# First attention of a two-block kernel: q and k in two float32r parts, 50 rows per head, two heads stacked on one array

## The chip, the cores and the metric

The kernel runs on one core of one Trainium2 chip. The metric is the device time of one execution in microseconds (us). Engines are named as the profile names them: PE (matmuls), PEld (PE's weight loads), DVE, ACT, POOL and SP, which issues most of the DMAs.

## What is computed

The input x has 8 images of 128 channels and 32 x 32 positions, so T = 1024 positions per image. The whole is an attention block, a mixture of experts, a convolutional linear attention and a second mixture of experts, each added to x. The change touches only the first attention and the stage that feeds it:

```python
xn = groupnorm(channelnorm(x))                 # [8, 128, 1024]
q, k, v = split(qkv_w @ xn + qkv_b, 3)         # 8 heads of 16 channels
q, k = q * scale, k * scale                    # scale = 1/2
weight = softmax(einsum('bct,bcs->bts', q, k)) # 64 heads, 1024 x 1024, float32
a = einsum('bts,bcs->bct', weight, v)
x = x + proj_w @ (xn + a) + proj_b
```

## The kernel before, in words

**Stages.** `metaformer` runs stages one after the other, with a barrier between two of them. `normalize_and_project` (from L51) makes q, k and v of every image and stores them to DRAM. `attend_and_route_first` (from L360) computes the attention and the routing of the first mixture. Experts, convolution, second routing and second mixture follow; the change leaves them as they are.

**Stage 1.** Per image, PE projects; ACT adds the bias to q and k (L184). Each is then split into three bf16 parts whose sum is the value to float32's accuracy: a copy on ACT gives the first part, a subtraction gives a rest (`split_rest`, L227; DVE has q, POOL has k), ACT copies the rest into the second part (L200), and a second subtraction, `split_last` (L232; again DVE q, POOL k), gives the third. ACT's L200 and `split_last` run in the next image's turn. DVE also copies v from the banks and normalizes. SP stores the parts (L109 to L113), 768 KB for each of q and k and image. Behind the first image's store, SP loads image 0's stacks from DRAM (L118), 12 transfers.

**The stacks.** A product of q and k in parts is a sum over six pairs of parts. `Q_PARTS` and `K_PARTS` list them (0,0), (0,1), (0,2), (1,0), (1,1), (2,0), and both operands hold them under each other: 6 x 16 = 96 rows (`KB`) of bf16, eight heads side by side on the free axis. Rows 96 to 98 (`KM` = 99) carry the row maxima: in `ks` they are ones, in `qs` the negated maximum of each query in three bf16 parts, so that a score leaves PE with its maximum already subtracted. POOL sets the ones (L1054) at the start of the attention stage.

**Two products.** A *maximum* (`take_max`, L550) multiplies 128 queries by 512 keys over 96 rows into a bank, and DVE's `reduce` (L779) takes the maximum over the keys. There are 256 units (8 heads, 8 chunks of queries, 2 halves of the keys) per image; after each 64 units DVE merges the halves and negates. PE transposes the result (`rows`, L543), DVE copies it (L789), POOL's `split_rows` (`split_in_three`, four operations, L40 to L48) makes the parts, and SP shifts them into `qs` (`max_rows`, L467, three transfers). A *score* (L652) is 128 keys by 512 queries over 99 rows; ACT takes the exponential of two of them at once (L726) into P; `weigh` (L632) multiplies P by v, eight float32 products on 32-column tiles of the array, two rounds of four heads.

**The order of the work.** The attention of one image is a body of 32 steps. Each step has two pairs of scores for two pairs of heads; behind each pair stand other units from the list `BODY_UNITS` (L326): this image's maxima from the 80th on, the next image's first 80 (`LEAD`), and for the image before the two projections (L557 and L559), the turns (L605), the logits (L611) and the ranks (L618). `STEP_OF` spreads the 264 units over the 32 steps by their place in the list. The first two units of a step come behind the first pair of scores, the others behind the second, and the weighing of the step before ends a step (L671). A unit takes one of three banks in turn, `slot = 5 + index % 3`, and waits until the unit three places ahead is done with it:

```python
pe.wait_ge(unit_freed, base + max(index - 2, 0))
```

Ahead of the first body the first 80 maxima run by themselves. SP loads the next image's stacks in two halves while a body runs (`load_qk`, L457).

Of the kernel before, what the change touches and what calls it, by code (L numbers as in the profile page):

```python
# [6 lines left out]
F32 = mybir.dt.float32  # L7
BF16 = mybir.dt.bfloat16
ALU = mybir.AluOpType
ACT = mybir.ActivationFunctionType  # L10
AX = mybir.AxisListType
# [10 lines left out]
Q_PARTS = (0, 0, 0, 1, 1, 2)  # L22
K_PARTS = (0, 1, 2, 0, 1, 0)
KB = len(Q_PARTS) * CH
KM = KB + 3
# [9 lines left out]
def split_in_three(eng, value, rest, parts, done, b, held=None):  # L35


    if held is not None:
        eng.sem_inc(held, 1)
    eng.tensor_copy(parts[:, 0], value).then_inc(done, 1)  # L40
    eng.wait_ge(done, b * 4 + 1)
    eng.tensor_tensor(rest, value, parts[:, 0], ALU.subtract).then_inc(done, 1)
    eng.wait_ge(done, b * 4 + 2)
    if held is not None:
        eng.sem_inc(held, 1)
    eng.tensor_copy(parts[:, 1], rest).then_inc(done, 1)
    eng.wait_ge(done, b * 4 + 3)
    eng.tensor_tensor(parts[:, 2], rest, parts[:, 1], ALU.subtract).then_inc(done, 1)  # L48


def normalize_and_project(nc, sb, sem, bank, w, X, XF, stacks0, parts_dram, v_dram):  # L51
# [9 lines left out]
    rest = sb("rest", [C, 2, T], F32)  # L61
    parts = sb("parts", [C, 2, 2, 3, T], BF16)
# [18 lines left out]
    first_parts, second_parts = sem("first_parts"), sem("second_parts")  # L81
    q_rest, k_rest, q_split, k_split = sem("q_rest"), sem("k_rest"), sem("q_split"), sem("k_split")
# [21 lines left out]
    with nc.Block() as block:  # L104
        @block.sync
        def _(sp):
# [10 lines left out]
            sp.wait_ge(parts_stored[0], 32)  # L117
            for r, (qp, kp) in enumerate(zip(Q_PARTS, K_PARTS)):  # L118
                for s, part, stack in ((0, qp, stacks0[0]), (1, kp, stacks0[1])):
                    sp.dma_start(stack[r * CH:(r + 1) * CH], parts_dram[0, s, part].rearrange("(h i) t -> i h t", i=CH)).then_inc(stacks_loaded, 16)  # L120
# [3 lines left out]
            sp.wait_ge(stacks_loaded, 16 * 2 * len(Q_PARTS))  # L124
# [48 lines left out]
        def _(act):  # L173
# [3 lines left out]
            def project(b, s):  # L177

                if s == 0:
                    act.wait_ge(q_rest, b)  # L180
                    act.wait_ge(k_rest, b)
# [5 lines left out]
            def step(db, b, nb, cb, p):  # L187
# [9 lines left out]
                if db is not None:  # L197
                    for s, rest_ready in enumerate((q_rest, k_rest)):
                        act.wait_ge(rest_ready, db + 1)
                        act.activation(parts[:, 1 - p, s, 1], rest[:, s], ACT.Copy).then_inc(second_parts, 1)  # L200
# [2264 lines left out]
```

## Time and profile before

| | before |
|---|---|
| median of 3 runs | 2270.06 us (2269.89 to 2271.42) |
| the profiled execution's own time | 2275.42 us |
| its span | 2273.5 us |
| mean granted clock of PE | 0.916 |
| PE busy | 1929.1 us, 85% of the span |
| PEld busy | 1073.3 us, 47% |
| DVE busy | 1436.2 us, 63% |
| ACT busy | 1098.7 us, 48% |
| POOL busy | 755.4 us, 33% |

The span is that of one execution taken by the profiler; what lies outside it is 1.9 us. Busy shares are means over stages with different limits, so a stage has to be read by itself. A busy PE counts matmuls whose records can overlap. The granted clock is a share of 2.4 GHz, 0.50 being 1.2 GHz. In the rows, "out<-in" gives the program's names, and the brackets behind a group are its idle time and what ended it.

### The profile page before, as it was taken

What the parts mean: (1) busy time and instruction counts of PE and PEld (TensorE: products, weight loads), DVE (VectorE), ACT (ScalarE), POOL (GpSimd) and SP (SyncE); (2) the same over time, 40 slices, a digit from 0 to 9 for tenths busy, and PEclk for the clock granted to TensorE, in tenths of its full rate; (3) what the DMA queues carried; (4) which work ended last, traced back from release to release, by engine and by line L of the source; (5) the groups of instructions that cost most, each with busy time, mean ns of one, the idle gap of its engine ahead of it and who ended that gap; (6) DMA issues with size and microseconds to landing.
All of it is one profiled execution on the core that took longest, in us unless ns stands there. A gap on an engine that the chain in (4) does not pass through costs nothing. (4 is left out here: it accounts for less than half of the span.)

```text
span 2273.5 us, 41046 instructions
## 1 busy us (share of the span) xinstructions
PE 1929.1 (85%) x13306; PEld 1073.3 (47%) x13307; DVE 1436.2 (63%) x3154; ACT 1098.7 (48%) x1682; POOL 755.4 (33%) x883
## 2 busy tenths in 40 slices
PE   5769999999999999998589996996659992699993
PEld 2331223332332323232367774554447661599992
DVE  4769888888888888871346665762235665344444
ACT  4550665666666666666144442541225551344442
POOL 0232003343333333345335553000001667355551
PEclk9875999999999999999699998999879996799995
DMA  3851532323232323012333333322100242233326
GB/s 127 193 217 33 78 55 29 60 35 65 31 66 29 66 29 66 2 38 63 105 86 99 95 99 119 111 84 61 38 29 29 62 136 81 71 94 92 90 72 229
DMA packets 134782, 180.00 MB, mean 79 GB/s; under 512 B 44592, under 2 KB 87856, under 8 KB 132336
## 3 DMA queue, kind: packets, MB, share of 16 engines
q1 hardware_dynamic: 116208, 138.25, 25.6%
q0 software_dynamic: 18432, 39.88, 5.2%
q8 instruction: 87, 1.43, 0.3%
q14 instruction: 55, 0.45, 0.1%
HBM read 99.04 MB, written 69.01 MB: 74 GB/s over the span
## 5 line engine op out<-in xcount | busy, mean ns | idle before, releaser
L779 DVE TENSOR_REDUCE mx<-bank 128x1 f32<-128x512 f32 x1024 | 639.7, 696 | 86.4 <-PE bank L550 85.2
L726 ACT ACTIVATE P<-bank 128x1024 f32<-128x1024 f32 x512 | 497.4, 1021 | 313.1 <-PE bank L652 312.9
L550 PE MATMUL bank<-ks,qs 96*128 96x512 bf16 x1024 | 358.6, 402 | 35.5 <-DVE mx L779 35.5
L1290 POOL DMA_INDIRECT results<-yo,places x284 | 274.1, 965 | 283.6 <-DVE yo L1280 236.8
L652 PE MATMUL bank<-qs,ks 99*128 99x512 bf16 x1024 | 308.2, 384 | 2.6 <-ACT P L726 1.8
L1206 PE MATMUL bank<-xt,up 128*128 128x256 f32 x1136 | 274.8, 386 | 3.7 <-DVE xt L1257 1.4
L632 PE MATMUL bank<-P,vt 128*32 128x512 f32 x2048 | 272.8, 605 | 0.7 <-ACT P L726 0.7
L2289 POOL DMA_INDIRECT dispatched<-planes,places x128 | 124.5, 973 | 420.2 <-DVE stats L2133 357.3
L1206 PEld LDWEIGHTS bank<-xt,up 128*128 128x128 f32 x1136 | 207.5, 193 | 30.4 <-issue 4.7
L550 PEld LDWEIGHTS bank<-ks,qs 96*128 96x128 bf16 x1024 | 99.8, 98 | 257.5 <-DVE mx L779 177.7
L652 PEld LDWEIGHTS bank<-qs,ks 99*128 99x128 bf16 x1024 | 78.0, 97 | 280.0 <-ACT P L726 182.8
L1237 ACT ACTIVATE hidden<-bank,rec 128x256 f32<-128x256 f32 x284 | 125.3, 473 | 144.3 <-PE bank L1206 144.3
L999 POOL TENSOR_TENSOR a<-o,den 128x512 f32<-128x512 f32 x32 | 40.6, 1268 | 381.4 <-ACT den L714 381.4
L1275 DVE TENSOR_TENSOR y<-bank,rec 128x256 f32<-128x256 f32 x142 | 60.3, 425 | 132.7 <-PE bank L1215 131.5
L1215 PE MATMUL bank<-planes,hidden 128*128 x1136 | 138.6, 276 | 0.7 <-DVE y L1275 0.7
L1049 POOL DMA_INDIRECT dispatched<-outgoing,places x128 | 123.8, 967 | 44.9 <-issue 39.9
L1215 PEld LDWEIGHTS bank<-planes,hidden 128*128 128x128 f32 x1136 | 132.5, 192 | 1.0 <-issue 0.9
L1717 PE MATMUL bank<-planes,bands 32*32 32x240 f32 (+2 forms) x3840 | 86.0, 396 | 41.6 <-issue 26.5
L1242 ACT ACTIVATE gate<-bank,rec 128x256 f32<-128x256 f32 x142 | 67.2, 473 | 111.1 <-PE bank L1206 111.1
L1738 DVE STREAM_TRANSPOSE planes<-out 128x1024 f32<-128x1024 f32 x24 | 43.6, 1894 | 98.6 <-ACT out L1730 98.6
L1189 PE MATMUL bank<-weights,xr 128*128 128x128 f32 x284 | 55.2, 277 | 47.8 <-DMA xr<-dispatched 47.1
L1269 DVE SCALAR_TENSOR_TENSOR hidden<-bank,rec,gate 128x256 f32<-128x256 f32 x142 | 68.6, 484 | 40.8 <-ACT gate L1242 31.0
(298 smaller groups left out, 2581.8 us busy)
## 6 DMA issues: line engine op xcount, KB each, us to landing
xr<-dispatched SPq DMA_DIRECT2D x142, 130.0 KB
qk_parts<-parts SPq DMA_DIRECT2D x16, 768.0 KB, 5.1
qs<-qk_parts SPq DMA_DIRECT2D x84, 128.0 KB
ks<-qk_parts SPq DMA_DIRECT2D x84, 128.0 KB
v_turned<-vt SPq DMA_DIRECT2D x8, 1024.0 KB, 5.6
vt<-v_turned SPq DMA_DIRECT2D x8, 1024.0 KB
bands<-results SPq DMA_DIRECT2D x32, 256.0 KB, 3.7
y<-results SPq DMA_DIRECT2D x32, 256.0 KB
```

What stands on the lines that cost most here:

```text
L550: pe.matmul(bank[:, slot, :], qs[par][0:KB, h, c * C:(c + 1) * C], ks[par][0:KB, h, half * HALF:(half + 1) * HALF], start=True, stop=True) ...
L632: ins = pe.matmul(bank[32 * j:32 * j + 32, 4, :], vt[:, par, s, head * VH:(head + 1) * VH], P[:, (2 * e + j // 2) % SLOTS, j % 2 * HALF:(j ...
L652: ins = pe.matmul(bank[:, 2 * pair + u, :], ks[par][:, head, s * C:(s + 1) * C], qs[par][:, head, n * HALF:(n + 1) * HALF], start=True, st ...
L726: act.activation(P[:, x % SLOTS, :], bank[:, 2 * pair:2 * pair + 2, :] .rearrange("p a t -> p (a t)"), ACT.Exp).then_inc(probs_ready, 1)
L779: dve.tensor_reduce(mx[:, k // 2, k % 2:k % 2 + 1], bank[:, slot, :], AX.X, ALU.max).then_inc(unit_freed, 1)
L1049: pool.indirect_dma_start(xd_dram, bass.IndirectOffsetOnAxis(places[:, q, k:k + 1], 0), outgoing[:, q, k, :], None).then_inc(sent, 16)
L1206: ins = pe.matmul(bank[:, 2 + f, 0:SLOT], up[:, p, f * C:(f + 1) * C], xt[:, p, :], start=True, stop=True)
L1215: ins = pe.matmul(bank[:, 6 + p, q * C:(q + 1) * C], hidden[:, p, f, q * C:(q + 1) * C], weights(e, W2 + f * C), start=(f == 0), stop=(f = ...
L1237: act.activation(hidden[:, p, f, :], bank[:, 2 + f, 0:SLOT], ACT.Gelu, bias=rec[:, r, f:f + 1]).then_inc(h_ready, 1)
L1290: pool.indirect_dma_start(yd_dram, bass.IndirectOffsetOnAxis(places[:, p, q:q + 1], 0), yo[:, p, q, :], None).then_inc(sent[p], 16)
L1717: ins = pe.matmul(sums[:, :, y0:y1], bands[rows, m * TAPS + dy, :], plane[:, :, y0 + dy - PAD:y1 + dy - PAD], start=(dy == DY_ORDER[0]), s ...
L2289: pool.indirect_dma_start(xd_dram, bass.IndirectOffsetOnAxis(places[:, p, q, k:k + 1], 0), rows[p][:, q, k, :], None).then_inc(sent[p], 16)
```

## The change

q and k are split into two parts in float32 storage, read as float32r by PE: the copy into the first part rounds to float32r, one subtraction gives the second. Three pairs of parts remain, 48 rows (`KB`) per head, and two rows of maxima make 50 (`KM`). One head's rows lie at partitions 0 to 49, the other's at 64 to 113 (`stack_rows`, `ROWS` = 64), so a stack has four pairs of heads on the free axis and 4096 float32 elements per partition where it had 8192 bf16. Maxima are counted so that units 2j and 2j + 1 are the same chunk of two stacked heads (`maximum`); `STEP_OF` goes by pairs, so both are in one step, and `first_half` puts two maxima or one other unit behind the first pair of scores. Each maximum still waits for its own unit's bank. Ones: stage 1's POOL sets those of one parity at its start, the attention's POOL the other's.

Stage 1 and the units, cut (lines "..." mark what is left out; the loads, the shifts and the waits on their counts change with the layout):

```diff
-Q_PARTS = (0, 0, 0, 1, 1, 2)
-K_PARTS = (0, 1, 2, 0, 1, 0)
+Q_PARTS = (0, 0, 1)
+K_PARTS = (0, 1, 0)
 KB = len(Q_PARTS) * CH
-KM = KB + 3
+KM = KB + 2
+PAIRS = HEADS // 2
+ROWS = C // 2
...
+    eng.tensor_copy(parts[:, 0].bitcast(F32R), value).then_inc(done, 1)
+    eng.wait_ge(done, b * 2 + 1)
+    eng.tensor_tensor(parts[:, 1].bitcast(F32R), value, parts[:, 0], ALU.subtract).then_inc(done, 1)
...
-    parts = sb("parts", [C, 2, 2, 3, T], BF16)
+    parts = sb("parts", [C, 2, 2, 2, T], F32)
...
+                    for u in range(2):
+                        sp.dma_start(stack[stack_rows(u, r)],
+                                     parts_dram[0, s, part].rearrange("(p u i) t -> u i p t", u=2, i=CH)[u]).then_inc(stacks_loaded, 16)
...
-                        act.activation(parts[:, 1 - p, s, 1], rest[:, s], ACT.Copy).then_inc(second_parts, 1)
...
-            eng.tensor_tensor(rest[:, s], qk[:, s], parts[:, p, s, 0], ALU.subtract).then_inc(rest_ready, 1)
-
-        def split_last(eng, s, b, p, split):
-
-            eng.wait_ge(second_parts, b * 2 + s + 1)
-            eng.tensor_tensor(parts[:, p, s, 2], rest[:, s], parts[:, p, s, 1], ALU.subtract).then_inc(split, 1)
+            eng.tensor_tensor(parts[:, p, s, 1].bitcast(F32R), qk[:, s], parts[:, p, s, 0], ALU.subtract).then_inc(ready, 1)
...
+            for u in range(2):
+                pool.memset(stacks0[1][u * ROWS + 32:(u + 1) * ROWS], 1.0).then_inc(ones_set, 1)
...
-    units.insert(units.index(("max", MAXIMA - 1)) + 4, ("rows", 1))
-    units.insert(units.index(("max", MAXIMA // 2 - 1)) + 4, ("rows", 0))
+    units.insert(units.index(("max", MAXIMA - 1)) + 3, ("rows", 1))
+    units.insert(units.index(("max", MAXIMA // 2 - 1)) + 3, ("rows", 0))
...
-STEP_OF = {unit: index * STEPS // len(BODY_UNITS) for index, unit in enumerate(BODY_UNITS)}
+BODY_GROUPS = [unit for unit in BODY_UNITS if unit[0] != "max" or unit[1] % 2 == 0]
+STEP_OF = {unit: index * STEPS // len(BODY_GROUPS) for index, unit in enumerate(BODY_GROUPS)}
+STEP_OF.update({("max", k): STEP_OF["max", k - 1] for k in range(1, MAXIMA, 2)})
...
+    pair, c, half, u = k // 32, k // 4 % TC, k // 2 % 2, k % 2
...
+    return 2 if now and now[0][1][0] == "max" else 1
...
-                pe.matmul(bank[:, slot, :], qs[par][0:KB, h, c * C:(c + 1) * C],
-                          ks[par][0:KB, h, half * HALF:(half + 1) * HALF], start=True, stop=True).then_inc(unit_filled, 1)
+                pe.matmul(bank[:, slot, :], qs[par][rows, pair, c * C:(c + 1) * C].bitcast(F32R),
+                          ks[par][rows, pair, half * HALF:(half + 1) * HALF].bitcast(F32R), start=True, stop=True).then_inc(unit_filled, 1)
...
-                            ins = pe.matmul(bank[:, 2 * pair + u, :], ks[par][:, head, s * C:(s + 1) * C],
-                                            qs[par][:, head, n * HALF:(n + 1) * HALF], start=True, stop=True)
+                            ins = pe.matmul(bank[:, 2 * pair + u, :], ks[par][rows_of, 2 * g + pair, s * C:(s + 1) * C].bitcast(F32R),
+                                            qs[par][rows_of, 2 * g + pair, n * HALF:(n + 1) * HALF].bitcast(F32R), start=True, stop=True)
...
-                        for index, (kind, k) in now[:2] if pair == 0 else now[2:]:
+                        for index, (kind, k) in now[:first_half(now)] if pair == 0 else now[first_half(now):]:
...
-                for par in range(2):
-                    pool.memset(ks[par][KB:KM, :, :], 1.0).then_inc(ones_set, 1)
-                pool.wait_ge(ones_set, 2)
+                for u in range(2):
+                    pool.memset(ks[1][u * ROWS + 32:(u + 1) * ROWS], 1.0).then_inc(ones_set, 1)
+                    pool.wait_ge(ones_set, u + 1)
```

How PE's instructions stand now, at two places. The first is the start of a body, its first two steps. Before, on PE (L652 scores, L550 maxima, L632 the weighing):

```order
L652 MATMUL bank<-qs,ks 128x512 x2
L550 MATMUL bank<-ks,qs 128x512 x2
L652 MATMUL bank<-qs,ks 128x512 x2
L550 MATMUL bank<-ks,qs 128x512 x3
L632 MATMUL bank<-P,vt 32x512 x4
L652 MATMUL bank<-qs,ks 128x512 x2
L550 MATMUL bank<-ks,qs 128x512 x2
L652 MATMUL bank<-qs,ks 128x512 x2
L550 MATMUL bank<-ks,qs 128x512 x2
L632 MATMUL bank<-P,vt 32x512 x4
```

and with the change, where scores are L659, maxima L559 and the weighing L641:

```order
L659 MATMUL bank<-qs,ks 128x512 x2
L559 MATMUL bank<-ks,qs 128x512 x2
L659 MATMUL bank<-qs,ks 128x512 x2
L559 MATMUL bank<-ks,qs 128x512 x4
L641 MATMUL bank<-P,vt 32x512 x4
L659 MATMUL bank<-qs,ks 128x512 x2
L559 MATMUL bank<-ks,qs 128x512 x2
L659 MATMUL bank<-qs,ks 128x512 x2
L559 MATMUL bank<-ks,qs 128x512 x2
L641 MATMUL bank<-P,vt 32x512 x4
```

The first step has six maxima where it had five: two behind the first pair of scores, four behind the second. The second step has four in both. Over a body the five-maxima steps, seven of them, become seven of six.

The second place is on PE around the projection (L557 and L559 before, L566 and L568 with the change). Before, an ordinary step and then both halves of the projection in one step:

```order
L652 MATMUL bank<-qs,ks 128x512 x2
L550 MATMUL bank<-ks,qs 128x512 x2
L652 MATMUL bank<-qs,ks 128x512 x2
L550 MATMUL bank<-ks,qs 128x512 x2
L632 MATMUL bank<-P,vt 32x512 x4
L652 MATMUL bank<-qs,ks 128x512 x2
L557 MATMUL bank<-XF,weights 128x512
L559 MATMUL bank<-a,weights 128x512 x2
L557 MATMUL bank<-XF,weights 128x512
L559 MATMUL bank<-a,weights 128x512 x2
L652 MATMUL bank<-qs,ks 128x512 x2
L550 MATMUL bank<-ks,qs 128x512 x2
```

and with the change:

```order
L659 MATMUL bank<-qs,ks 128x512 x2
L559 MATMUL bank<-ks,qs 128x512 x2
L659 MATMUL bank<-qs,ks 128x512 x2
L566 MATMUL bank<-XF,weights 128x512
L568 MATMUL bank<-a,weights 128x512 x2
L641 MATMUL bank<-P,vt 32x512 x4
L659 MATMUL bank<-qs,ks 128x512 x2
L566 MATMUL bank<-XF,weights 128x512
L568 MATMUL bank<-a,weights 128x512 x2
L659 MATMUL bank<-qs,ks 128x512 x2
L559 MATMUL bank<-ks,qs 128x512 x2
L641 MATMUL bank<-P,vt 32x512 x4
```

The two halves of the projection stand in two neighbouring steps, each beside one pair of maxima, where both were in one step with two maxima behind them.

## Rows read from the trace of the kernel before

**Rows 1.** Windows: bounds, us; busy of PE, PEld, DVE, ACT, POOL; clock; DMA share; GB/s.

```profile
20.00:168.00 148.00, 104.19 (x271) 55.29 (x270) 102.24 (x168) 84.01 (x128) 35.36 (x16) 0.82 0.56 163
180.00:221.00 41.00, 40.55 (x70) 7.20 (x69) 40.97 (x71) 0.00 (x0) 3.52 (x5) 0.50 0.03 7
221.00:1056.00 835.00, 802.08 (x4339) 248.49 (x4338) 672.79 (x1312) 550.28 (x633) 269.28 (x397) 1.00 0.29 47
1556.00:1582.00 26.00, 18.85 (x895) 12.77 (x895) 4.15 (x3) 5.12 (x5) 0.00 (x0) 1.00 0.28 77
```

**Rows 2.** Groups of instructions, 220 to 1060 us: busy, mean ns of one | idle before.

```profile
L779 DVE TENSOR_REDUCE mx<-bank 128x1 f32<-128x512 f32 x949 | 590.6, 683 | 85.7 <-PE bank L550 84.4
...
L550 PE MATMUL bank<-ks,qs 96*128 96x512 bf16 x947 | 313.7, 385 | 30.2 <-DVE mx L779 30.2
L652 PE MATMUL bank<-qs,ks 99*128 99x512 bf16 x1024 | 308.2, 384 | 2.6 <-ACT P L726 1.8
...
L550 PEld LDWEIGHTS bank<-ks,qs 96*128 96x128 bf16 x946 | 91.5, 97 | 215.4 <-DVE mx L779 136.2 <-issue 0.6
...
L611 PEld LDWEIGHTS bank<-router,X 128*128 128x128 f32 x112 | 13.1, 192 | 0.0
```

**Rows 3.** Timeline of one ordinary step and one with five maxima: start, length, engine, group.

```profile
425.21 0.61 PE L652 MATMUL bank<-qs,ks 99*128 99x512 bf16 x2
...
425.65 0.60 PE L550 MATMUL bank<-ks,qs 96*128 96x512 bf16 x2
...
426.07 2.49 DVE L779 TENSOR_REDUCE mx<-bank 128x1 f32<-128x512 f32 x4 [0.44 <-PE bank L550]
...
426.82 0.10 PEld L550 LDWEIGHTS bank<-ks,qs 96*128 96x128 bf16 x1 [0.41 <-DVE mx L779]
...
427.14 1.07 PE L632 MATMUL bank<-P,vt 128*32 128x512 f32 x8
...
428.14 0.61 PE L652 MATMUL bank<-qs,ks 99*128 99x512 bf16 x2
...
429.04 3.08 DVE L779 TENSOR_REDUCE mx<-bank 128x1 f32<-128x512 f32 x5 [0.48 <-PE bank L550]
...
431.71 0.39 PE L652 MATMUL bank<-qs,ks 99*128 99x512 bf16 x1
```

**Rows 4.** Timeline of PE around the projection, turns and logits of a body.

```profile
557.88 0.60 PE L652 MATMUL bank<-qs,ks 99*128 99x512 bf16 x2
558.32 1.02 PE L557 MATMUL bank<-XF,weights 128*128 128x512 f32 x2
...
560.89 1.02 PE L557 MATMUL bank<-XF,weights 128*128 128x512 f32 x2
...
565.43 0.61 PE L652 MATMUL bank<-qs,ks 99*128 99x512 bf16 x2
...
571.88 0.60 PE L652 MATMUL bank<-qs,ks 99*128 99x512 bf16 x2
...
576.63 0.60 PE L652 MATMUL bank<-qs,ks 99*128 99x512 bf16 x2
```

**Rows 5.** Groups of the page: the convolution's products on 32 x 32 tiles.

```profile
L1717 PE MATMUL bank<-planes,bands 32*32 32x240 f32 (+2 forms) x3840 | 86.0, 396 | 41.6 <-issue 26.5
```

**Rows 6.** Groups of instructions, 0 to 170 us: the copies and subtractions of stage 1.

```profile
L232 POOL TENSOR_TENSOR parts<-rest,parts 128x1024 bf16<-128x1024 f32 x8 | 17.1, 2136 | 33.8 <-ACT parts L200 33.8
...
L200 ACT ACTIVATE parts<-rest 128x1024 bf16<-128x1024 f32 x16 | 16.0, 1049 | 20.9 <-DVE rest L227 20.9
...
L232 DVE TENSOR_TENSOR parts<-rest,parts 128x1024 bf16<-128x1024 f32 x8 | 9.7, 1217 | 1.1 <-ACT parts L200 1.1
```

**Rows 7.** DMA issues, 60 to 168 us: loads of image 0's stack, KB each, us to landing.

```profile
qs<-qk_parts SPq DMA_DIRECT2D x6, 256.0 KB, 15.2
```

**Rows 8.** Timeline at the start of the attention stage, 168 to 176 us.

```profile
168.32 13.81 POOL L1054 MEMSET ks<- 3x8192 bf16 x2 [6.12 <-POOLq L2319]
...
168.39 6.88 DVE L880 COPY base<-weights 128x8 f32<-128x8 f32 x1 [8.17 <-PEq L2319]
```

More of the change, by code:

```diff
@@ L8 @@
 BF16 = mybir.dt.bfloat16
+F32R = mybir.dt.float32r
 ALU = mybir.AluOpType
@@ L272, in step @@
                     copy_v(b, p, 1)
-                if db is not None:
-                    split_last(dve, 0, db, 1 - p, q_split)
                 if nb is not None:
@@ L289, in step @@
                     copy_v(b, p, 3)
-                    split_rest(dve, 0, b, p, q_rest)
+                    split(dve, 0, b, p, q_split)
             over_images(dve, step)
@@ L339, with maximum, first_half @@
 BODY_UNITS = units_of_a_body()
-STEP_OF = {unit: index * STEPS // len(BODY_UNITS) for index, unit in enumerate(BODY_UNITS)}
+BODY_GROUPS = [unit for unit in BODY_UNITS if unit[0] != "max" or unit[1] % 2 == 0]
+STEP_OF = {unit: index * STEPS // len(BODY_GROUPS) for index, unit in enumerate(BODY_GROUPS)}
+STEP_OF.update({("max", k): STEP_OF["max", k - 1] for k in range(1, MAXIMA, 2)})
+def maximum(k):
+    pair, c, half, u = k // 32, k // 4 % TC, k // 2 % 2, k % 2
+    return pair, c, half, u
+def first_half(now):
+    return 2 if now and now[0][1][0] == "max" else 1
 def of_next(unit):
@@ L463, in max_rows @@
             def max_rows(b, par, g):
-                sp.wait_ge(rows_split, b * 8 + 4 * g + 4)
-                for part in range(3):
-                    sp.dma_start(qs[par][KB + part:KB + part + 1, 4 * g:4 * g + 4, :]
-                                 .rearrange("p h (c t) -> p (h c) t", t=C),
-                                 nm_parts[:, part, :]).then_inc(rows_loaded, 16)
+                sp.wait_ge(rows_split, b * 4 + 2 * g + 2)
+                for u in range(2):
+                    for part in range(2):
+                        row = u * ROWS + KB + part
+                        sp.dma_start(qs[par][row:row + 1, 2 * g:2 * g + 2, :].rearrange("p h (c t) -> p (h c) t", t=C),
+                                     nm_parts[16 * u:16 * u + 16, part, :]).then_inc(rows_loaded, 16)
             def blank_rows_at(sp, n):
@@ L545, in take_max @@
             def take_max(b, par, k, slot):
-                h, c, half = k // 16, k // 2 % TC, k % 2
+                pair, c, half, u = maximum(k)
+                rows = slice(u * ROWS, u * ROWS + KB)
                 if k % 64 == 0:
                     pe.wait_ge(qk_loaded[k // 64], b * LOADS)
-                pe.matmul(bank[:, slot, :], qs[par][0:KB, h, c * C:(c + 1) * C],
-                          ks[par][0:KB, h, half * HALF:(half + 1) * HALF], start=True, stop=True).then_inc(unit_filled, 1)
+                pe.matmul(bank[:, slot, :], qs[par][rows, pair, c * C:(c + 1) * C].bitcast(F32R),
+                          ks[par][rows, pair, half * HALF:(half + 1) * HALF].bitcast(F32R), start=True, stop=True).then_inc(unit_filled, 1)
             def project(b, n, slot):
@@ L778, in reduce @@
                 dve.wait_ge(unit_filled, filled)
-                dve.tensor_reduce(mx[:, k // 2, k % 2:k % 2 + 1], bank[:, slot, :], AX.X, ALU.max).then_inc(unit_freed, 1)
+                pair, c, half, u = maximum(k)
+                row = 32 * (pair // 2) + 16 * u + 8 * (pair % 2) + c
+                dve.tensor_reduce(mx[:, row, half:half + 1], bank[:, slot, :], AX.X, ALU.max).then_inc(unit_freed, 1)
                 if k % 64 == 63:
@@ L2339, in metaformer @@
             with ExitStack() as first:
-                stacks0 = [allocator(first, nc.sbuf_tensor)(name, [KM, HEADS, T], BF16)[:] for name in ("qs0", "ks0")]
+                stacks0 = [allocator(first, nc.sbuf_tensor)(name, [C, PAIRS, T], F32)[:] for name in ("qs0", "ks0")]
                 stage(normalize_and_project, X, XF, stacks0, parts_dram, v_dram)
```

70 lines of the change are left out of this document (28 added, 42 removed).

## Prediction

> **What bounds the kernel now.** I read the table by stretches first [rows 1]. The first attention is its third line: from 221 to 1056 us, 835 of the 2273.5 us. There PE is busy for 802 us, DVE for 673, ACT for 550, at a granted clock of 1.00. A busy PE is no proof, since matmul records overlap, so I went on to the groups of instructions [rows 2] and to one step in the order of time [rows 3].
>
> An ordinary step (four scores L652, four maxima products L550, the weighing L632 of the step before) goes from 425.21 to 428.14 us: 2.93 us. DVE's four reductions take 2.49 of it. What sets its length is a chain through both engines [rows 3]: first scores at 425.21; first maximum product 0.44 later (two scores at 0.22); DVE starts 0.42 after that; the weight load of the fourth maximum product, which waits until the first reduction has freed its bank, another 0.75 later (426.82); the weighing 0.32 later; the next scores 1.00 later. 0.44 + 0.42 + 0.75 + 0.32 + 1.00 = 2.93. The scores of the second pair and the third maximum product lie beside the first reduction and cost nothing. A step with five maxima lasts 3.57: one more reduction of 0.60.
>
> **The change, part by part.** The sum is made against the profiled execution, 2275.42 us with a span of 2273.5; the median of the runs, 2270.06, is 5.4 lower.
>
> *Ordinary steps.* Each score and each maximum product now has 50 or 48 rows in float32r and a head's half of the array, heads in turn. I take one float32r product to stream as a bf16 one, 0.22 us, and the two of a pair to run beside each other. The nearest row for the second is the convolution, whose 3840 products on small tiles of the array are busy for 86.0 us together, 22 ns each against 396 ns of one [rows 5]; no run here shows it for halves. Of the chain only the first pair of scores gets shorter, by 0.22. Against it stands the weight load: one of 128 bf16 columns reads 97 ns, one of 128 f32 columns 192 [rows 2], and in two places of the chain nothing hides it: at the first scores after the weighing (other tile shape) and at the maximum that waits. I take the f32 row, since the elements have four bytes: 2 x 0.095 = 0.19. So 2.93 - 0.22 + 0.19 = 2.90, almost nothing. Ends: a load as short as bf16's gives 2.71; loads of a pair one after the other add another 0.10, 3.00.
>
> *Steps laid out anew.* Maxima now keep together in pairs, so a step has six where it had five. By the order a body had seven steps of five maxima, twenty of four, one of four with a transposition, and four with other units; now it has seven of six, eighteen of four, one of four with a transposition, and six with other units. A sixth reduction adds 0.60: 3.57 becomes 4.14, seven times +0.57 = +4.0. Eighteen ordinary steps at -0.03: -0.5. The projection had 2.93 + 7.55 with one ordinary step [rows 4]; now it has two steps, each 0.32 + 0.22 + 0.22 for the pairs, 2.57 for three f32 products (558.32 to 560.89), 1.00 for the weighing and two changes of tile shape at about 0.1: 4.5, together 9.0, so -1.5. Turns and logits had 4.75 + 2.93; now I estimate 2.8 and 3.9, -1.0. The two steps with a transposition or the ranks lose one product and two halves, about three times 0.2 each: -1.1. Sum per image 4.0 - 0.5 - 1.5 - 1.0 - 1.1 = -0.1. What a body gains where PE is the limit it loses in the steps of six, where DVE is. With eight bodies I put the attention at 0; by the ends of the load, in some 22 steps per image and 7.5 bodies' worth of images, -31 to +17.
>
> In that sum stand about 0.1 us for each change of tile shape. From the weighing's start to the next scores 1.00 us go by [rows 3], for two rounds of f32 products that stream 0.43 each (2.57 for six records [rows 4]), so 0.14 is left for two changes. The Trainium skill, TensorEngine Tiling (Array Packing), Key Properties, speaks against this change here: "Changing tiling mode (not just tile) drains the TensorE", and the halves are a third mode between full-array units and weighing. The trace agrees with those 0.14; without that rule some 16 new changes per image would cost nothing and the sum would be about 12 us lower.
>
> *The 80 maxima ahead of the first body* come at one per 0.60 us, DVE is busy for 40.97 of 41 us [rows 1]: PE's part is covered, 0.
>
> *The stage before (20 to 168 us).* Per image fall away two ACT copies (16 of 1.05 us in all), a DVE subtraction of 1.22 and a POOL one of 2.14 [rows 6]. The DVE subtraction stands between copies of v and the next image's normalization: I count it for seven images, 8.5 us. The ACT copies and POOL's lie mostly beside PE's projection and count 0 there, but behind the last image the third part (copy 2.0, POOL 2.1) is gone: -4.3, less 1 for a store of 1024 instead of 768 KB. Together -12. Ends: with the copies too on the path -20; the stores bring 16 x 256 KB = 4.2 MB more, which at 163 GB/s for a DMA share of 0.56 [rows 1], some 290 GB/s when full, would take 14 us if nothing hid them: +2. The loads of the stacks move the same bytes as before in twelve transfers, half as many and longer packets; they take 15 us each when queued together [rows 7], and I leave that.
>
> *Ones.* Ahead of the first maxima POOL sets two times 3 x 8192 bf16 elements in 13.81 us, and DVE's first copy, 128x8, lasts 6.88, as long as the first of them [rows 8]. Now it is 4096 f32 elements for one parity in two pieces; at the same time per element 3.5 each, so DVE starts 3.4 earlier: -3.4 (0 to -6.9). The other parity's are set in the stage before while DVE still waits for x.
>
> *Loads inside the bodies* keep their bytes, at a DMA share of 0.29 [rows 1]; the rows of maxima go in four transfers instead of three, after two POOL operations instead of four. Hidden, and less than 1 us if not.
>
> Sum: 0 - 12 - 3.4 = -15.4, so 2275.42 becomes 2260.0, and the median 2270.06 becomes **2255**. The likeliest case's own range is 2230 to 2275.
>
> The Trainium skill, FP8 and Floating Point Precision, TensorE Precision Notes, has reduced-precision FP32 truncated to 22 bits and only true FP32 in four passes. By that 0.22 us per product holds; no run here shows it.
>
> **Rivals.**
> 1. *The load is hidden or short* (chance 0.15). The array may load a half while the other streams, as the convolution's loads do. Then ordinary steps take 2.71, -31: 2224. Against it: the 192 ns row, and two places where no product is ahead.
> 2. *The halves don't run beside each other* (0.12). Then each pair takes 0.44 as before, and the longer load is paid without the gain: +0.22 in 22 steps and some 1.5 in the others, +6.3 per image, 47 in all: 2302, slower than before. It decides once the second product of a pair starts more than 0.09 us behind the first (15.4 us over 22 x 7.5 steps). For it: no 64-row tile in the trace. Against it: [rows 5].
> 3. *A float32r product streams like one f32 record*, 0.43 us (0.07). First scores and the waiting maximum each add 0.21, about 11.5 per image with the other steps, 86 in all: 2341.
> 4. *The clock stays low* (0.06). From 180 to 221 us, with one product per 0.60 us, 0.50 was granted (1.2 GHz) all along [rows 1]; the bodies lifted it. With fewer streaming columns the first body might not. A step then takes about 1.4 more (weighing 1.0, products 0.4); 30 steps are +42: 2297. Against it: the convolution keeps 1.00 with PE busy for 18.85 of 26 us [rows 1], 72%, and a step would have four pairs of 0.22 and the weighing's 1.00 in 2.90, 66%: a little less, so it isn't ruled out, but its gaps are short. The Trainium skill, TensorE: Matmul & The Clock Gate, Part 1, also has activity release a throttled clock; the trace agrees by these two stretches.
> 5. *Nothing on the path* (0.10): the stores take back what the first stage gains, steps stay at 2.93, and only the ones count: 2267.
>
> **How the numbers follow.** About 0.2%, 4.5 us, is what a measurement of this kernel tells from no change. The likeliest case has 0.50: 0.41 faster, 0.06 same, 0.03 slower. With rival 1 faster (0.15), 2, 3 and 4 slower (0.25), and rival 5 split in 0.01, 0.07 and 0.02: faster 0.57, same 0.13, slower 0.30. The range goes from 2215, rival 1 with some more of the first stage, to 2305, rival 2; it leaves out rival 3 and the far parts of the others, less than 2 in 10.
>
> **What would show it.** Right: ordinary steps of 2.85 to 2.95 us, steps of six maxima near 4.1, weight loads of the halves near 190 ns, the two scores of a pair starting within 0.02 us and the first maximum some 15 us earlier. Wrong: loads near 100 ns and steps of 2.7 (rival 1); a second score 0.2 behind the first (2); products that follow each other at 0.43 with a granted clock of 1.00 (3); 0.50 granted inside a body (4); a stage before the attention that still ends at 168 us (5).

## The result, and the profile after

The changed kernel took 2365.97 us (median of 4 runs, 2339.27 to 2379.02) where the kernel before took 2270.74: 4.2% more. The ratio, 1.0335 with a 95% interval of 1.0269 to 1.0401, is that of the two faster runs (2339.27 and 2356.02); the two slower ones, of which the profiled one is the slowest, lie over 1.5% above the fastest. The forecast was 2255 with a range of 2215 to 2305, so time and sign were both missed. The four runs lie further apart than those of the kernel before, and their mean granted clocks go with their times: 0.875, 0.868, 0.853 and 0.849 from the fastest to the slowest, where the kernel before has 0.916. The profiled execution took 2379.02 us, with a span of 2377.2; all lines and counts below are of it.

A correction first: the description of the kernel before counts 256 maxima per image and 264 units in the list. There are 128 (8 heads, 8 chunks, 2 halves; 1024 records for 8 images) and 136. The step counts of the sum were taken from the order of the instructions and are not touched by it.

The page of the changed kernel: PE's busy time, and the granted clock in 40 slices.

```profile
PE 2024.6 (85%) x13306; PEld 1174.3 (49%) x13307; DVE 1418.6 (60%) x3146; ACT 1085.1 (46%) x1666; POOL 728.4 (31%) x845
...
PE   5879999999899999999868999698658995499994
...
PEclk9966877678988897959969999899988997699995
```

Slices 4 to 20 are the attention. PE is busy for eight or nine tenths of each, but the clock stands at 5 to 9 tenths. The same by a window, from the first step of the first body to the last of the last (columns as in [rows 1]):

```profile
197.00:1165.00 968.00, 903.03 (x4339) 338.97 (x4337) 675.06 (x1312) 552.56 (x633) 259.01 (x367) 0.81 0.23 40
```

Where [rows 1] had 835 us at 1.00 there are now 968 at 0.81. DVE and ACT are busy for the same time as before. What an ordinary step looks like at the high clock, on PE, PEld and DVE (L659 scores, L559 maxima, L641 the weighing, L788 the reductions):

```profile
302.90 0.49 PE L659 MATMUL bank<-qs,ks 50*128 50x512 f32 x2
...
303.23 0.40 PE L559 MATMUL bank<-ks,qs 48*128 48x512 f32 x2
...
303.67 2.48 DVE L788 TENSOR_REDUCE mx<-bank 128x1 f32<-128x512 f32 x4 [0.46 <-PE bank L559]
...
304.41 0.18 PEld L559 LDWEIGHTS bank<-ks,qs 48*128 48x128 f32 x1 [0.75 <-DVE mx L788]
...
304.84 1.07 PE L641 MATMUL bank<-P,vt 128*32 128x512 f32 x8
...
305.84 0.50 PE L659 MATMUL bank<-qs,ks 50*128 50x512 f32 x2
```

This is the chain of [rows 3] again: 0.33 + 0.44 + 0.74 + 0.43 + 1.00 = 2.94 us. The same step at the low clock:

```profile
403.71 0.79 PE L659 MATMUL bank<-qs,ks 50*128 50x512 f32 x2
...
404.31 0.62 PE L559 MATMUL bank<-ks,qs 48*128 48x512 f32 x2
...
404.97 2.48 DVE L788 TENSOR_REDUCE mx<-bank 128x1 f32<-128x512 f32 x4 [2.10 <-PE bank L559]
...
406.44 1.93 PE L641 MATMUL bank<-P,vt 128*32 128x512 f32 x8
...
408.30 0.79 PE L659 MATMUL bank<-qs,ks 50*128 50x512 f32 x2
```

It takes 4.59 us, 1.65 more. DVE's four reductions still last 2.48, but DVE now waits 2.10 for PE: the weighing takes 1.93 instead of 1.07. The weighing tells the clock of each step, so I counted, of the 256 weighings of the profiled execution, those that lasted over 1.45 us: none before, 78 now.

A fall, on PE in the timeline, around a step of six maxima:

```profile
349.83 0.50 PE L659 MATMUL bank<-qs,ks 50*128 50x512 f32 x2
350.17 0.40 PE L559 MATMUL bank<-ks,qs 48*128 48x512 f32 x2
350.41 0.40 PE L659 MATMUL bank<-qs,ks 50*128 50x512 f32 x2
350.65 0.39 PE L559 MATMUL bank<-ks,qs 48*128 48x512 f32 x1
351.35 1.69 PE L559 MATMUL bank<-ks,qs 48*128 48x512 f32 x3 [0.32 <-DVE mx L788]
352.97 1.64 PE L641 MATMUL bank<-P,vt 128*32 128x512 f32 x8
354.54 0.80 PE L659 MATMUL bank<-qs,ks 50*128 50x512 f32 x2
```

From 350.65 to 352.97 PE issues four maxima and waits for DVE between them; the weighing behind them takes 1.64, so the clock dropped while it ran, and the next scores read 0.80 instead of 0.50. Of the 26 low stretches of the run, 22 begin like this one, in a step of six (0, 4, 8, 12, 16, 20, 24) or directly behind one, or in or behind step 18, in which PE waits for DVE's routing (1.84 us at once in the second body); three begin in the step with the logits, and one is the start.

**Where the 103.7 us between the two spans are.** The fourth reduction of the attention (its rows stand below, with the ones) starts at 151.50 instead of 176.02 us: -24.5 (the first of all starts at 148.40 instead of 169.40). From there to the start of the last step it is 1011.3 us instead of 877.8: +133.5. What follows is 5.3 us shorter, which I leave. Of the 133.5, the new layout at the high clock has 2.3 us per image, about 18 (the medians of the steps at 1.00 add up to 110.2, with steps 21 and 22, which never ran at 1.00 from end to end here, taken at 2.94 and 2.65 from the runs below; before, 107.9). The clock has the rest, about 115; 78 weighings in steps that are 1.65 longer would be up to 129. In the fastest run, 40 us shorter at a higher mean clock, its part is presumably smaller; its trace was not kept.

### The profile page after: what moved, and what is told of

Same layout as the page of the kernel before. It is cut to its first block and busy times, and to the rows that moved or that the text cites. A ratio compares the mean times of both kernels' runs of the same rounds, so it can differ in the third digit from the quotient of the medians.

```text
span 2377.2 us, 40967 instructions
## 1 busy us (share of the span) xinstructions
PE 2024.6 (85%) x13306; PEld 1174.3 (49%) x13307; DVE 1418.6 (60%) x3146; ACT 1085.1 (46%) x1666; POOL 728.4 (31%) x845
## 5 line engine op out<-in xcount | busy, mean ns | idle before, releaser
L788 DVE TENSOR_REDUCE mx<-bank 128x1 f32<-128x512 f32 x1024 | 635.0, 686 | 191.6 <-PE bank L559 189.3
L559 PE MATMUL bank<-ks,qs 48*128 48x512 f32 x1024 | 408.3, 529 | 62.7 <-DVE mx L788 52.3
L641 PE MATMUL bank<-P,vt 128*32 128x512 f32 x2048 | 339.8, 742 | 0.8 <-ACT P L733 0.7
L559 PEld LDWEIGHTS bank<-ks,qs 48*128 48x128 f32 x1024 | 184.5, 234 | 230.4 <-DVE mx L788 218.5
L659 PE MATMUL bank<-qs,ks 50*128 50x512 f32 x1024 | 279.9, 543 | 4.0 <-ACT P L733 4.0
L659 PEld LDWEIGHTS bank<-qs,ks 50*128 50x128 f32 x1024 | 116.5, 224 | 306.8 <-issue 184.5
```

The costliest lines, as they stand in the source:

```text
L559: pe.matmul(bank[:, slot, :], qs[par][rows, pair, c * C:(c + 1) * C].bitcast(F32R), ks[par][rows, pair, half * HALF:(half + 1) * HALF].bit ...
L641: ins = pe.matmul(bank[32 * j:32 * j + 32, 4, :], vt[:, par, s, head * VH:(head + 1) * VH], P[:, (2 * e + j // 2) % SLOTS, j % 2 * HALF:(j ...
L659: ins = pe.matmul(bank[:, 2 * pair + u, :], ks[par][rows_of, 2 * g + pair, s * C:(s + 1) * C].bitcast(F32R), qs[par][rows_of, 2 * g + pair ...
L788: dve.tensor_reduce(mx[:, row, half:half + 1], bank[:, slot, :], AX.X, ALU.max).then_inc(unit_freed, 1)
```

## Experiments

Steps of five, steps of six: the layout of before and that of the change. "Low" is the number of weighings over 1.45 us. The times are medians of all runs of a kernel. Clock, busy share and "low" are of its one profiled execution, clock and share in the window of all bodies. Each ratio is to the kernel before as run beside it.

| kernel | products | layout | median us | clock | PE busy | low |
|---|---|---|---|---|---|---|
| before | bf16, 96 and 99 rows | five | 2270.74 | 1.00 | 96% | 0 |
| change | f32r, 48 and 50, pairs | six | 2365.97 | 0.81 | 93% | 78 |
| e1 | as before | six | 2293.81 | 0.99 | 95% | 3 |
| e2 | as the change | five | 2274.11 | 0.96 | 89% | 14 |
| e3 | f32r, 48 and 50, one by one | six | 2459.74 | 0.77 | 92% | 92 |
| e4 | as the change, maxima doubled | six | 2355.44 | 0.85 | 97% | 59 |
| e5 | bf16, 48 and 50, pairs | six | 2235.45 | 0.91 | 88% | 38 |
| e6 | bf16, 48 and 50, one by one | six | 2321.36 | 0.89 | 87% | 39 |
| e7 | as the change, steps filled | five | 2256.50 | 0.98 | 91% | 6 |
| e8 | e7, logits apart | five | 2301.57 | 0.93 | 92% | 26 |
| e9 | e7, step 9 filled too | five | 2259.66 | 0.97 | 91% | 12 |
| e10 | bf16, 48 and 51, one by one | five | 2684.61 | 0.60 | 99% | 182 |
| e11 | as the change, scores 64 rows | six | 2329.82 | 0.89 | 91% | 45 |
| e12 | e7, scores 64 rows | five | 2246.89 | 0.99 | 91% | 1 |

**The layout alone (e1).** The kernel before with the new grouping:

```diff
+BODY_GROUPS = [unit for unit in BODY_UNITS if unit[0] != "max" or unit[1] % 2 == 0]
+STEP_OF = {unit: index * STEPS // len(BODY_GROUPS) for index, unit in enumerate(BODY_GROUPS)}
+STEP_OF.update({("max", k): STEP_OF["max", k - 1] for k in range(1, MAXIMA, 2)})
...
+                        for index, (kind, k) in now[:first_half(now)] if pair == 0 else now[first_half(now):]:
```

> The kernel before (bf16, 96 and 99 rows, products one after the other) with only the new layout of units: seven steps of six maxima per image, the projection in two steps. Stage 1 is that of before. Theory A (the side-by-side pairs): in a step PE now has less to do, stands idle longer and loses its clock; without the pairs this kernel keeps a granted clock of 1.00 in the bodies and takes 2270 to 2290. Theory B (the layout): PE loses its clock in the steps of six, where it waits for DVE; then low stretches come here too and the time is 2320 or more.

It took 2293.81 us, a ratio of 1.0094 (1.0077 to 1.0111), a little over theory A's range. Its bodies:

```profile
220.00:1080.00 860.00, 816.23 (x4343) 248.44 (x4344) 673.80 (x1312) 550.28 (x633) 269.92 (x397) 0.99 0.28 46
```

The same waits for DVE, with steps of six at 4.12 us, leave the clock at 0.99: so the layout alone (theory B) does not lower it. A body takes 110.35 at the high clock, 2.4 more than before, so the layout has a price of its own.

**The pairs alone (e2).** The changed kernel with `STEP_OF` by single units, `rows` four places behind and the first two units behind the first scores:

```diff
-    return 2 if now and now[0][1][0] == "max" else 1
+    return 2
```

> The changed kernel with the layout of units of before: seven steps of five maxima, twenty of four, the projection in one step; float32r pairs stay. Theory A: the clock still falls inside the bodies, 2310 to 2365. Theory B: the clock stays at 1.00 in the bodies; stage 1 and the ones give the 24.5 us that the changed kernel's profile shows ahead of the first maximum, a body takes about 107 us, so 2240 to 2250.

It took 2274.11 us (2264.56 to 2283.92, 10 runs), between the two theories' ranges: ratio 1.0006 (0.9985 to 1.0028). A body at the high clock takes 107.9 us, as before; three of the four falls behind its start begin in step 18, which takes 4.46 us. The steps of six are the larger part of the loss, but only together with these products: with bf16 products of 96 rows, in e1, the clock drops next to nothing.

**One product after the other (e3).** Consecutive products take the same half of the array:

```diff
-    pair, c, half, u = k // 32, k // 4 % TC, k // 2 % 2, k % 2
+    pair, c, half, u = k // 32, k // 4 % TC, k % 2, k // 2 % 2
...
-                            rows_of = slice(u * ROWS, u * ROWS + KM)
-                            ins = pe.matmul(bank[:, 2 * pair + u, :], ks[par][rows_of, 2 * g + pair, s * C:(s + 1) * C].bitcast(F32R),
+                            rows_of = slice(pair * ROWS, pair * ROWS + KM)
+                            ins = pe.matmul(bank[:, 2 * pair + u, :], ks[par][rows_of, 2 * g + u, s * C:(s + 1) * C].bitcast(F32R),
```

> The changed kernel, but the two products that follow each other are of the same half of the array (two heads of the upper half, then two of the lower; two key halves of one head's maximum), so they stream one after the other; float32r, 50 rows, loads and steps of six stay. Theory A: PE is busy for longer in each step and keeps the clock; the first pair of scores costs 0.2 us more per step, so 2290 to 2310 with a clock of 1.00 in the bodies. Theory B: the steps of six still drop the clock, over 2340. Theory C (the half array or the type counts less whatever PE does): the clock falls, over 2360.

2459.74 us (2419.55 to 2489.0), the clock at 0.77:

```profile
199.00:1264.00 1065.00, 981.76 (x4344) 382.43 (x4347) 675.80 (x1312) 556.59 (x633) 259.67 (x368) 0.77 0.19 37
```

Theory A falls here. PE has more to stream one after the other than in the changed kernel, and the clock is not higher. Nor is it clearly lower: the mean clocks of the runs, 0.822 to 0.856, overlap those of the changed kernel, and part of the longer time is longer steps (2.97 to 3.17 us for an ordinary one at 1.00). Theory C, that the half array or the type counts for less, is what is left.

**Doubled maxima (e4).**

```diff
+                for _ in range(again):
+                    pe.matmul(bank[:, slot, :], qs[par][rows, pair, c * C:(c + 1) * C].bitcast(F32R),
+                              ks[par][rows, pair, half * HALF:(half + 1) * HALF].bitcast(F32R), start=True, stop=True)
...
+                                         1 if pair == 1 and index != now[-1][0] else 0)
```

> The changed kernel with work added: each maximum behind the second pair of scores, but for the step's last, is issued twice into the same bank (the first without a signal), about 110 products more per image, all where PE waits for DVE. Theories A and B: the clock stays at 1.00 or nearly, an ordinary step stays at 2.94 and one of six at 4.14, and the time falls to 2255 to 2275, close to or below the kernel before. Theory C: the clock falls as in the changed kernel, and the time is 2340 to 2380 or more.

2355.44 us (2345.01 to 2364.74), a ratio of 1.0351 (1.0325 to 1.0378): the same as the changed kernel within the noise, and far from 2275. It added 40 products per image, not 110 (there are 128 maxima, as said above). PE is busy for 97% of the window, more than in the kernel before, at 0.85. The share of busy time does not decide. A low clock itself raises that share, since products then last longer (0.79 us for two scores instead of 0.50), so the column mixes cause and effect; e10 separates them.

**The type (e5, e6).** The changed kernel and e3 in bf16, with q, k and the maxima to some 16 bits:

```diff
-    parts = sb("parts", [C, 2, 2, 2, T], F32)
+    parts = sb("parts", [C, 2, 2, 2, T], BF16)
...
-                pe.matmul(bank[:, slot, :], qs[par][rows, pair, c * C:(c + 1) * C].bitcast(F32R),
+                pe.matmul(bank[:, slot, :], qs[par][rows, pair, c * C:(c + 1) * C],
```

> The changed kernel with bf16 in place of float32r: two bf16 parts (so q, k and the maxima keep some 16 bits), the same 48 and 50 rows, halves, pairs and steps of six; stage 1 stores half the bytes. Weight loads fall to about 0.10 us and an ordinary step at 1.00 to 2.7 to 2.75 us. Theory D (float32r products hold the clock less than bf16 ones): the clock stays at 1.00 in the bodies but for a few dips, as in the bf16 kernel with steps of six, and the time is 2225 to 2250. Theory E (products of 48 rows on half the array hold it less, whatever their type): low stretches as in the changed kernel, 250 us or more of them in the bodies, and 2320 to 2370.

> The kernel with half-array products one after the other, in bf16 as the run beside it. Per step PE streams as many columns one after the other as the kernel before does, in the same type; only the rows per product are 48 and 50 where they were 96 and 99. Theory D: clock 1.00 in the bodies but for a few dips, 2255 to 2285. Theory E: the clock falls as in the float32r kernel of this kind, 400 us or more low, and over 2380.

2235.45 us (2234.44 to 2245.86) and 2321.36 (2305.54 to 2331.37). The clocks are 0.91 and 0.89, with 38 and 39 low weighings where float32r had 78 and 92 and the bf16 kernel of 96 rows, e1, had 3. So neither theory alone: the kernels of few rows lose the clock in bf16 too, and float32r makes it worse. In e5 and e6 a fall is over after one to three weighings in most cases and after six at most; in the changed kernel it lasts up to 14. Whether the type itself does that, or its longer weight loads, these runs don't tell. e5 is also about the price of the loads: an ordinary step at 1.00 takes 2.70 us with loads of 93 ns, 2.94 with float32r's 187 ns. At 2235 it is faster than every kernel here, but with less of q and k.

**Full-array work where PE waits (e7).**

```diff
+FILLED = (18, 20)
...
+                            if pair == 1 and e in FILLED and index == now[first_half(now)][0]:
+                                pe.matmul(bank[:, slot, :], vt[:, par, s, 0:C], P[:, 2 * (e - 1) % SLOTS, 0:HALF], start=True, stop=True)
```

> The float32r pairs with the old layout (steps of five), and one product added in steps 18 and 20 of each body, where PE waits for DVE's routing: 128 columns of v by 512 of P in float32, on all 128 rows, into the bank of the third maximum ahead of that maximum, which overwrites it. In the run without it the low stretches all begin behind step 18. If PE's idleness there brings the clock down: no low stretch in the bodies, a body of 108 to 109 us, and 2245 to 2253 with a narrow spread. If the clock falls for another reason (float32r or few rows throughout): stretches as before, 2262 to 2284.

2256.50 us (2245.84 to 2267.21), a ratio of 0.9926 (0.9898 to 0.9955), where e2 without the products has 1.0006 (0.9985 to 1.0028). With one product of 128 rows in each of two steps of a body, no fall begins in or behind steps 18 and 20; these steps keep their 4.45 and 4.48 us. Three falls behind the start remain, all in step 10, which holds the turns and the logits, and where the profiled execution of e2 had none. The time lies between the two ranges expected.

**Step 10 (e8, e9).**

```diff
-    units[44:44] = [("turn", 0), ("turn", 1), ("logits", 0)]
+    units[44:44] = [("turn", 0), ("turn", 1)]
+    units[50:50] = [("logits", 0)]
```

> The filled kernel with steps of five, and the logits moved four units later in the list, so that step 10 has two maxima and the two turns, and step 11 three maxima and the logits (in the run before, step 10 held the turns and the logits, which have 8 columns a product, and the three dips that were left in its bodies all came at its end). If thin stretches of PE bring the clock down, no dip is left: body 107.5 to 108.5 us, 2243 to 2250 and a spread under 10 us. If not: dips stay, and 2246 to 2267 as before this move.

```diff
-FILLED = (18, 20)
+FILLED = (9, 18, 20)
```

> The filled kernel with steps of five and a third added product, in step 9 ahead of the step with the turns and the logits. It lies in a step of 2.94 us where PE has 0.4 us to spare, so 0.4 to 0.6 us on the path per image, 3 to 5 in all. If the dip behind step 10 depends on what PE did ahead of it: no dips, 2247 to 2255. If it depends on step 10 alone: dips stay, 2249 to 2271.

With the logits apart, 2301.57 us (2293.47 to 2311.63), over both ranges: step 10 takes 3.69 us but step 11 takes 5.43 or more, longer than the logits had been beside the turns (4.95), and the clock falls in it or behind it in all seven bodies that hold logits. With step 9 filled, 2259.66 us (2249.19 to 2265.29), the expectation's second case: the falls in step 10 stay, so what PE does just ahead of it does not prevent them. No run fills step 10 itself.

**Rows alone (e10).** The kernel before, its layout, its type, its place on the array, with three pairs of parts instead of six:

```diff
-Q_PARTS = (0, 0, 0, 1, 1, 2)
-K_PARTS = (0, 1, 2, 0, 1, 0)
+Q_PARTS = (0, 0, 1)
+K_PARTS = (0, 1, 0)
...
+            pool.memset(stacks0[1][32:KM], 1.0).then_inc(ones_set, 1)
```

> The kernel before, in its own layout and with bf16 products one after the other on the same place of the array, with one thing changed: three pairs of parts in place of six, so 48 and 51 rows per product where it had 96 and 99 (q, k keep some 16 bits; stage 1 is that of before, the loads of the stacks are half). No step gets shorter or longer by its own chain: 2.93. If the rows of a product count for the clock: low stretches behind steps 18 to 20 and more, 2285 to 2320. If only how long PE stands idle counts: clock 1.00 in the bodies and 2260 to 2270 (half the loads, a shorter set of ones).

2684.61 us (2627.64 to 2709.7), 16 to 19% above the kernel before and far over the range expected if rows count. The second body of e10, steps 8 to 18 and what follows, by windows:

```profile
437.60:475.80 38.20, 35.66 (x204) 11.65 (x200) 33.70 (x78) 25.36 (x32) 15.85 (x23) 1.00 0.17 23
477.00:577.00 100.00, 100.00 (x304) 22.89 (x303) 52.62 (x92) 40.89 (x44) 16.51 (x27) 0.50 0.12 25
```

and the same in the kernel before:

```profile
349.60:387.30 37.70, 35.10 (x204) 12.15 (x200) 33.79 (x78) 25.36 (x32) 15.87 (x23) 1.00 0.20 26
387.30:427.00 39.70, 38.10 (x215) 11.36 (x211) 34.31 (x65) 25.87 (x29) 6.38 (x18) 1.00 0.16 18
```

With the same 204 products and PE busy for 93% of the time in both, the clock falls behind step 18 in e10 and stays in the kernel before. A later low stretch of e10 and the end of it:

```profile
640.00:740.00 100.00, 100.00 (x304) 22.90 (x303) 51.02 (x85) 40.48 (x44) 20.45 (x31) 0.50 0.13 28
746.00:760.00 14.00, 13.79 (x62) 4.43 (x60) 9.26 (x16) 6.01 (x7) 0.00 (x0) 0.99 0.00 0
```

and on PE at that end (L658 scores, L556 maxima, L638 the weighing, L563 and L565 the projection):

```profile
740.70 1.93 PE L638 MATMUL bank<-P,vt 128*32 128x512 f32 x8
742.57 1.03 PE L658 MATMUL bank<-qs,ks 51*128 51x512 bf16 x2
743.53 2.07 PE L563 MATMUL bank<-XF,weights 128*128 128x512 f32 x2
745.39 2.38 PE L565 MATMUL bank<-a,weights 128*128 128x512 f32 x4
747.61 1.02 PE L563 MATMUL bank<-XF,weights 128*128 128x512 f32 x2
748.46 1.88 PE L565 MATMUL bank<-a,weights 128*128 128x512 f32 x4
750.28 0.60 PE L658 MATMUL bank<-qs,ks 51*128 51x512 bf16 x2
```

This is the clearest run of the study. At the high clock an ordinary step is that of before (2.92 us). In the low stretch PE is busy for 100.00 of 100 us, without a pause that a record shows, and the clock stays at 0.50. It rises within the projection, products of all 128 rows, and not before; the other low stretches of e10 end at a projection too. One thing was changed in the products: how many rows they read. So the rows count, and the time that PE is busy does not decide by itself.

**More rows at no time (e11, e12).** A score product reads 64 rows of its half; those added are zeros in q's stack and ones in k's:

```diff
-                            rows_of = slice(u * ROWS, u * ROWS + KM)
+                            rows_of = slice(u * ROWS, (u + 1) * ROWS)
```

> The changed kernel with one thing changed: a score product reads all 64 rows of its half (the 14 rows added are zeros in q's stack and ones in k's, so the result is the same); maxima keep 48. Every instruction, step and wait stays as in the changed kernel; two memsets of 3.5 us each come to POOL ahead of the first rows. If the rows that a product reads hold the clock, whatever they hold, the low stretches get shorter: 2310 to 2350. If rows of zeros don't count, or if the half of the array is what matters and not its rows: 2340 to 2380 as the changed kernel.

> The same added rows in the filled kernel with steps of five (products added in steps 18 and 20), the fastest of the float32r kernels so far. If rows of any content count: the dips behind step 10 go, 2244 to 2252 with a narrow spread. If not: 2246 to 2267 as before.

Both came out in the range for rows of any content. The changed kernel goes from 2365.97 to 2329.82 us (2323.66 to 2334.71, all below its fastest run), with 45 low weighings instead of 78; by the ratios it is 1.0237 (1.0217 to 1.0257) instead of 1.0335 (1.0269 to 1.0401), about 1%. The filled kernel of steps of five comes to 2246.89 (2240.42 to 2252.87): a ratio of 0.9883 (0.9865 to 0.9901), faster than the kernel before by 1.2% with the parts and products of the change. Its bodies:

```profile
195.00:1033.00 838.00, 759.32 (x4382) 296.02 (x4381) 675.74 (x1318) 550.51 (x633) 259.71 (x368) 0.99 0.26 47
```

The only low weighing is the first of the first body, where the clock rises, and from body to body it is 99.0 us and then six times 107.9, as before. PE is busy for 91%, less than in any of the kernels with the clock at 0.85 and lower. Rows that are zeros on one side count too: e11 shows it by times that don't overlap. e12 agrees, but by itself it is not clear of e7, whose interval (0.9898 to 0.9955) overlaps its own.

## Why the prediction was wrong

**Ordinary steps: right.** 2.90 was the sum, 2.94 is what they take at the high clock. The two scores of a pair start 3 ns apart (225 before), so the halves do run beside each other, and the weight loads read 187 ns, as taken from the f32 row of [rows 2]. The other end, 2.71 with loads as short as bf16's, is what e5 shows: 2.70.

**Steps laid out anew: mechanism right, sum 2.4 us per image too low.** Steps of six take 4.13 (4.14 in the sum), the projection 4.67 + 4.86 instead of 9.0, turns and logits 3.03 + 3.97 instead of 2.8 + 3.9, the step at a body's start 4.28 instead of 4.14. At the high clock a body is 2.3 us longer, not 0.1 shorter.

**The stage before: right in sign, too small.** The stage of the attention starts at 147.0 instead of 168.3 us: -21.3, where -12 was the sum and -20 the end of the range. ACT of before, and of the change, in the timeline of that stage:

```profile
63.77 2.00 ACT L200 ACTIVATE parts<-rest 128x1024 bf16<-128x1024 f32 x2 [2.48 <-DVE rest L227]
...
77.95 2.00 ACT L200 ACTIVATE parts<-rest 128x1024 bf16<-128x1024 f32 x2 [2.48 <-DVE rest L227]
```

```profile
72.08 2.42 ACT L186 ACTIVATE qk<-bank,bqk 128x512 f32<-128x512 f32 x4 [0.99 <-DVE parts L224]
...
83.44 2.42 ACT L186 ACTIVATE qk<-bank,bqk 128x512 f32<-128x512 f32 x4 [0.99 <-DVE parts L224]
```

These images take 11.4 us instead of 14.2. The copies L200 had been counted at nothing, as lying beside PE's projection; but ACT reached them only behind a wait of 2.48 for DVE, and the copies of q and k out of PE's banks stood behind them. They were on the path, 2.0 us each image. The subtraction ahead of them on DVE takes part of that back: it lasts 2.47 us instead of 1.21. The larger stores (7.3 us to land instead of 5.1) cost little: ACT's one long wait for a store is 10.4 us instead of 8.7.

**The ones: right.** The start of the attention's stage in the changed kernel:

```profile
147.03 7.07 POOL L1063 MEMSET ks<- 32x4096 f32 x2 [9.49 <-POOLq L2328]
...
147.10 3.46 DVE L889 COPY base<-weights 128x8 f32<-128x8 f32 x1
...
151.50 36.57 DVE L788 TENSOR_REDUCE mx<-bank 128x1 f32<-128x512 f32 x61 [0.92 <-PE bank L559]
```

and the reductions of the kernel before, from the fourth on, as in the last line above:

```profile
176.02 36.56 DVE L779 TENSOR_REDUCE mx<-bank 128x1 f32<-128x512 f32 x61 [0.75 <-PE bank L550]
```

DVE's first copy lasts 3.46 instead of the 6.88 of [rows 8]: -3.4, as summed (-3.2 at the fourth reduction). The 80 maxima still come one per 0.60 us.

**The clock: this is the step that failed.** The sum takes every step of the attention at the clock of 1.00 and has no term for it; in the profiled execution the clock was 0.81 there and cost about 115 us. Rival 4 had it, with a chance of 0.06, a price of 42 us and a place in the first body alone. Its price per step, 1.4 us, was near the 1.65 measured; its 30 steps were not near the 78. Two things in its working were wrong. It weighed PE's busy share: 72% in the convolution of [rows 1] kept 1.00, a step here would have 66%, "a little less", so little was feared. But in e10 and in the kernel before PE is busy for 93% of the same steps at 1.00, and only e10 falls behind them; and e12 keeps 0.99 with 91%. So this share does not tell by itself, and the rows that the products read count. The change halves them; e5 and e6 against the float32r kernels show that the type, or its longer loads, adds to it. And it took the clock for a matter of the start, where a body either lifts it or not; in fact it falls and rises in every body, with 26 low stretches in the profiled run, and every fall but the first begins where PE waits for DVE or runs thin products. [rows 1] had half of the warning: a stretch, 180 to 221 us, that PE spends at 0.50 with 40.55 of 41 us busy. That the rows count, no row of the kernel before shows.

The Trainium skill, TensorE: Matmul & The Clock Gate, Part 1, was cited there for activity that releases a throttled clock, and says that the gate goes by "how busy the PE has been recently". The trace agrees that it falls behind thin stretches. That a PE busy for 100 of 100 us stays at 0.50 in e10 differs from that sentence, if "busy" is read as the busy time of the profile, and the measurement decides.

**The sign.** Without the clock the sum would have been -24.5 + 18, so some 2269 from the profiled 2275.42: a few microseconds faster, and not the 15 of the forecast. With the steps of five, two added products per body and filled rows, which hold the clock, e12 is 27 us faster than the kernel before; its bodies take as long, so nearly all of it lies ahead of the first body.

## What to carry to other kernels

Before halving the rows of PE's products, count the rows as well as the time: packing two products side by side saves streaming time, but where the engine then waits for another, the clock can fall and cost more than the packing gains. A granted clock of 1.00 in every body of the kernel before did not show how near it was to falling; look at the rows of its products, and at the steps in which PE waits. Here rows of zeros against ones left the steps at the high clock as long as they were (2.94 and 4.13 us), and so did one full-array product in a step with a long wait (4.45 us); both held the clock longer. The same product in a step without such a wait cost 0.44 us (e9: 3.38 instead of 2.94). A layout that collects waits into fewer, longer ones can cost more than its own step times say: with these products, steps of six cost some 90 us against e2, of which the steps at the high clock explain 18.

## What was not expected of the hardware

- The kernel of before with half the rows per product and nothing else in its steps changed went from a clock of 1.00 to 0.60 in the bodies, from 2274 to 2685 us, with PE busy for 99% of the time.
- Fourteen added rows per score product, zeros against ones, took 36 us off the median of the changed kernel (1% by the ratios), and the profiled execution of the filled one has no fall left.
- Two float32r products on two halves of the array start 3 ns apart (median) and end within the time of one, 0.50 us together at the high clock.
- Why the bf16 kernel that takes one half of the array for two products and then the other (e6) climbs out of a fall in a few steps, while the one that always reads the same rows of the array (e10) stays low for 20 to 38 of them until the projection, is open: its steps are also laid out differently.
